# Spline attention: the exponents of a row block in two pieces of 1568 columns instead of four of 784

## The reference, cut to what matters

```python
q, k, v = (x projected by Wq, Wk, Wv)          # 4 heads of 32, 3136 pixels
sim  = einsum('bhnd,bhdm->bhnm', q, k) / sqrt(32)
xs   = clip(sim, -6, 6)
kan  = base_w * silu(xs) + einsum('...k,k->...', b_splines(xs), coef)   # cubic splines, knots 2.4 apart
attn = softmax(kan, axis=-1)                   # over the 3136 keys
out  = einsum('bhnm,bhmd->bhnd', attn, v)
return einsum('bihw,ci->bchw', out, Wo)
```

## Time and profile before

| what | value |
|---|---|
| median of three runs | 8487.42 us |
| profiled execution, its own time | 8486.63 us |
| its span | 8484.9 us |
| busy share PE / DVE / ACT / POOL | 79% / 77% / 69% / 64% |
| mean granted TensorE clock | 0.916 |

### The profile page before, as it was taken

The page is one execution under the profiler, slowest core; times in us unless marked ns, Lnnn a source line. Parts: engine busy times, 40 slices in busy tenths (PEclk is TensorE's granted clock), DMA queues, the critical chain, the costliest instruction groups (busy, mean ns, idle before and its releaser), DMA issues. The chain is left out here.

```text
span 8484.9 us, 160875 instructions
## 1 busy us (share of the span) xinstructions
PE 6665.1 (79%) x52568; PEld 4066.2 (48%) x52568; DVE 6493.4 (77%) x8488; ACT 5894.8 (69%) x8624; POOL 5438.2 (64%) x3590
## 2 busy tenths in 40 slices
PE   5676689989678888876888888688888867888886
PEld 3444447767544444443444444344444434444443
DVE  3323374444489999987999999499999969999997
ACT  4325002223189999986999899399999958999996
POOL 3314000000088888876888888388888858888885
PEclk7788799999899999998999999799999989999998
DMA  1000000000100000001000000200000010000001
GB/s 64 17 11 27 0 0 0 0 0 0 47 8 0 0 0 0 0 2 29 0 0 0 0 0 0 62 1 0 0 0 0 0 31 1 0 0 0 0 0 39
DMA packets 44706, 72.18 MB, mean 9 GB/s; under 512 B 8928, under 2 KB 40448, under 8 KB 42016
## 3 DMA queue, kind: packets, MB, share of 16 engines
q1 hardware_dynamic: 41296, 70.25, 3.1%
q10 hardware_dynamic: 3288, 0.33, 0.0%
HBM read 50.69 MB, written 19.73 MB: 8 GB/s over the span
## 5 line engine op out<-in xcount | busy, mean ns | idle before, releaser
L1389 POOL TENSOR_TENSOR a_s<-a_s,a_v 128x784 f32<-128x784 f32 x1568 | 2910.2, 1857 | 568.2 <-ACT a_s L1563 521.3
L1425 PE MATMUL a_right_sides<-a_s,diag_d 128*128 128x392 f32 x6272 | 2470.5, 541 | 233.3 <-DVE a_prob L1470 212.8
L1425 PEld LDWEIGHTS a_right_sides<-a_s,diag_d 128*128 128x128 f32 x6272 | 1237.0, 210 | 1074.3 <-issue 420.0
L1497 DVE SCALAR_TENSOR_TENSOR a_kan<-a_s,spline_c,a_kan 128x784 f32<-128x784 f32 x1568 | 1629.5, 1039 | 112.4
L1437 PE MATMUL a_turned<-ident,a_prob 128*112 128x128 f32 x5488 | 937.3, 296 | 854.0 <-ACT a_probT L1570 661.2
L1382 POOL TENSOR_TENSOR a_inner<-a_inner,a_x 128x784 f32<-128x784 f32 x784 | 1453.8, 1854 | 65.4
L1437 PEld LDWEIGHTS a_turned<-ident,a_prob 128*112 128x112 f32 x5488 | 584.3, 138 | 1116.4 <-ACT a_probT L1570 718.2
L1546 ACT ACTIVATE a_a<-a_x 128x784 f32<-128x784 f32 x784 | 672.2, 857 | 509.6 <-DVE a_x L1476 506.8
L1449 PEld LDWEIGHTS a_weighed<-a_probT,a_V 112*64 112x64 f32 x21952 | 755.8, 138 | 491.2 <-issue 434.8
L1449 PE MATMUL a_weighed<-a_probT,a_V 112*64 112x64 f32 x21952 | 945.9, 229 | 0.2
L1507 DVE CUSTOM_DVE_ANT_0 a_prob<-a_kan,a_prob 128x784 f32<-128x784 f32 x784 | 764.1, 975 | 153.9 <-DVE a_kan L1497 153.9
(11 more groups left out here) (182 smaller groups left out, 7840.0 us busy)
## 6 DMA issues: line engine op xcount, KB each, us to landing
rows<-bias_rows_dram SPq DMA_DIRECT2D x112, 91.0 KB
X<-in_x_dram SPq DMA_DIRECT2D x4, 1568.0 KB, 15.0
v_dram<-V SPq DMA_DIRECT2D x14, 448.0 KB, 3.1
a_K<-k_dram SPq DMA_DIRECT2D x8, 784.0 KB, 9.5
QO<-q_dram SPq DMA_DIRECT2D x8, 784.0 KB, 12.8
a_V<-v_dram SPq DMA_DIRECT2D x4, 1568.0 KB, 22.1
f_R<-rinv_dram SPq DMA_DIRECT2D x8, 784.0 KB, 7.6
out_dram<-X SPq DMA_DIRECT2D x4, 1568.0 KB, 10.2
```

The costliest lines, as they stand in the source:

```text
L1389: eng.tensor_tensor(s, s, v, ALU.mult).then_inc(cubed, 1)
L1425: mm = eng.matmul(up[:, j, 0:SUB], steps[i][:, :], cubes[g][:, SUB * j:SUB * (j + 1)], start=(i == 0), stop=(i == 1))
L1497: eng.scalar_tensor_tensor(F, banked((s1, s2)[j][g][:, :]), c[:, 3 + j:4 + j], F, ALU.mult, ALU.add).then_inc(left_added, 1)
```

## The change: what it does

The list of ScalarE has two exponents a step instead of four. `exponent(half)` works on 1568 columns, the quarters 2 x half and 2 x half + 1 of `prob`, and adds 2 to `exp_done`, so that all waits keep their numbers. `exponent(1)` stands where the exponent of quarter 2 stood, `exponent(0)` where that of quarter 0 stood; the entries of quarters 3 and 1 are gone.

```diff
-                def exponent(g):
+                def exponent(half):
                     def stage(eng, t, r):
+                        f = prob[r][:, HALF * half:HALF * (half + 1)]
                         eng.wait_ge(max_ready, t + 1)
-                        eng.activation(part(r, g), part(r, g), ACT.Exp, bias=nmax[r][:, :]).then_inc(exp_done, 1)
+                        eng.activation(f, f, ACT.Exp, bias=nmax[r][:, :]).then_inc(exp_done, 2)
                     return stage
...
-                pipeline(act, TILES3, [(tanh(2), 1), (copies(1), 2), (first_knot(0), 0), (exponent(2), 2), (copies(2), 2), (second_knot(0), 0),
-                                       (tanh(3), 1), (copies(3), 2), (first_knot(1), 0), (exponent(3), 2), (copies(4), 2), (second_knot(1), 0),
+                pipeline(act, TILES3, [(tanh(2), 1), (copies(1), 2), (first_knot(0), 0), (exponent(1), 2), (copies(2), 2), (second_knot(0), 0),
+                                       (tanh(3), 1), (copies(3), 2), (first_knot(1), 0), (copies(4), 2), (second_knot(1), 0),
                                        (tanh(0), 0), (copies(5), 2), (first_knot(2), 0), (exponent(0), 1), (copies(6), 2), (second_knot(2), 0),
-                                       (tanh(1), 0), (copies(0), 1), (first_knot(3), 0), (exponent(1), 1), (place, 2), (second_knot(3), 0)])
+                                       (tanh(1), 0), (copies(0), 1), (first_knot(3), 0), (place, 2), (second_knot(3), 0)])
```

## The result

The changed kernel takes 8520.37 us, the median of six runs (8515.73 to 8523.13), against 8487.19 us before (six runs, 8485.32 to 8491.7): ratio 1.0038, 95% interval 1.0025 to 1.0051, 33 us slower. The forecast was 8549 us, 62 slower, with a range of 8500 to 8595. The profiled execution took 8517.76 us, its span is 8516.0 us, 31.1 more than before.

What follows compares the result with a forecast made beforehand. VectorE was taken to bound the spline attention. Two waits of L1484 (47 us) and the late copy (15 us) made 62 us, so 8487.4 + 62 = 8549 us, with a range of 8500 to 8595.

Steps and rivals of the forecast that it cites:

- What bounds: Spline attention: VectorE is full, ScalarE waits for it; VectorE's work alone makes the block of 29.39 us.
- The saving: ScalarE's exponents: a 1568-column piece takes 1596 ns; 0.36 us less per block, in idle time, counted at nothing.
- ScalarE's wait before Abs: Sign for the profile after: ScalarE's wait before Abs, 509.6 us idle before the change, would be larger.
- The two waits of L1484: VectorE's first addition waits for a later TANH, 0.17 us in quarter 3, 0.08 to 0.09 in quarter 1: 47 us.
- The copy behind TANH of quarter 3: ScalarE's later copy delays TensorE's right side and, in some blocks, TANH of quarter 1: 15 us, from 0 to 60.
- the 19 of the working: Blocks, of 196, in which the prediction saw ScalarE wait for TensorE at the later copy.
- the assumed quarter of all blocks: Share of blocks in which the late copy would delay TANH of quarter 1: 50 x 0.3 = 15 us.
- The waits for right sides: VectorE's waits for TensorE's right sides: near 47.5 us still, over 100 if the clock case is right.
- the late square and cube of quarter 2: ScalarE's second square and GpSimd's cubes are 0.66 us late; additions wanting the cubes come more than a quarter later.
- Hidden: Rival: the margin before L1484 absorbs the longer exponent, 8487 to 8504 us; chance 0.14.
- ScalarE's saving: Rival: ScalarE sets the step, so 0.36 us a block, 71 us, would go: 8417 us; chance 0.04.
- The clock: Rival: TensorE's gap grows from 1.62 to about 2.1 us, lowering its clock; 91 us on top, 8640 us; chance 0.14.

Runs made afterwards that it cites:

- e10b: e7b with pieces of 1008, 1232 and 896 columns, so that the transpose of chunk 2 waits for the second piece: 9372.69 us.
- e1: Kernel before with only the first half as one exponent of 1568 columns; quarters 2 and 3 keep their own: 8487.65 us.
- e2: Kernel before with only the second half as one exponent of 1568 columns; quarters 0 and 1 keep their own: 8508.13 us.
- e3b: Changed kernel with each half as two exponents of 784 columns directly behind each other: 8592.55 us.
- e4: Changed kernel with both exponents of 1568 columns moved ahead of first_knot, where ScalarE would wait for the clip: 8492.04 us.
- e9b: e7b with its first piece moved ahead of first_knot(2): 8490.9 us.
- e7b: Changed kernel with three pieces cut at transposed chunks' edges: 1344 columns at quarter 0's old place, 896 at those of quarters 2 and 3: 8461.55 us.
- e12: e7b with its first 1344 columns as 1008 and 336, so four pieces (1008, 336, 896, 896) at the four old places: 8473.28 us.
- e5: Kernel before with its four exponents of 784 columns each moved ahead of first_knot: 8488.59 us.
- e11b: e7b's three pieces in the kernel before, plus the copy of chunk 1 moved ahead of the TANH of quarter 2: 8496.07 us.
- e6b: Changed kernel with second_knot(2) moved ahead of the exponent of the first half: 8546.72 us.

## Why the prediction was right, and what in it was not

**What bounds.** Right. VectorE has next to no idle time to give in the stages. Every kernel here but e10b is its work plus these two sorts of waits, to within 4 us over the stages.

**The saving.** Right: L1581 takes 1587 ns for the 1596 forecast, and the time saved went into idle time, that before TANH (51.8 us before, 254.1 after). One sign named ahead was wrong: ScalarE's wait before Abs was to be larger and is smaller, 476.8 us for 509.6.

**The two waits of L1484.** Right, and they are the result: 0.17 us forecast for quarter 3 and 0.165 measured, 0.09 for quarter 1 and 0.086 measured. 47 us were forecast and 51.3 measured; the difference is mostly the 30 blocks left out as held before, which were not held any more. The sign was stated in the wrong measure: as idle time the 40 to 50 us forecast are 21.0, as start-to-start time 51.3. e1 and e2 show either half by itself, e3b the same sum at 0.84 us, e4 and e9b that nothing is left of it where the exponent stands before the clip's wait.

**The copy behind TANH of quarter 3.** This step failed, 15 us forecast. In 11 blocks L1484 of quarter 1 was over 0.1 us later than in the others, 2.1 us in all. In the kernel before ScalarE waited at that copy in 11 blocks and not in the 19 of the working, and none came on top, so the assumed quarter of all blocks was 50 for 11.

**What wasn't in the sum.** The waits for right sides were taken as fixed ("near 47.5 us still"), and they went, 18 us. I had the late square and cube of quarter 2 in the working and looked only for whom they hold up, which is TensorE (104.8 us of waits) but never VectorE through it. That heavy work placed later might keep TensorE's clock up just after was not asked.

**The time.** It came out at 33 us for 62, just over half: 15 us too much for the copy and 18 for the waits that went, against 4 too few for L1484. The direction and the larger term are right by their mechanism.

**The rivals.** Hidden fell with e3b and both halves. ScalarE's saving fell: e4 has the shorter ScalarE and no late TANH, and is at 1.0001; the rule of the Trainium skill ("ScalarE: Activation LUTs", section on what ACT_TABLE_LOAD costs) holds for the instruction (1587 ns for 1568 columns, 933 for 784) and not for the step. The clock mattered, but the other way. The gap before the right side of quarter 0, on which this rival stood, did not grow to 2.1 us: where it is long it is about 1.6 us before and after, and the waits before that gate did not grow at all. The Trainium skill ("TensorE: Matmul & The Clock Gate", section on HAM oscillation) warns of idle gaps between bursts of matmuls. That gaps matter the trace bears out, though the gaps of that section's example are longer than the 1.6 to 2.2 us here. But of the two here only the one before quarter 3 cost something, and the longer gap did not cost the more: before its transpose TensorE is idle 1.85 us (median) in the kernel before, with 30 waits, and 2.16 in the changed one, with 2.

**Still open.** Theory D rests on the swap of e9b, on e7b, and on the times of e12; it is a rule found in this kernel, and how the clock decides is not shown. The time from the end of the right side of quarter 2 to the start of that of quarter 3 goes with it in the main: 5.38 to 5.43 us (medians) in the kernel before, e4, e5 and e9b, with 23 to 36 waits, 4.67 to 4.76 in the changed kernel, e1, e3b and e7b, with 2. But e12 has 5.05 with 17 waits and e2 5.24 with 12, so it is not the whole. That e2 has 12 waits and not 30, with an early cube, is not explained. e7b and e12 are 9 and 7 us faster than their account; over the stages of the profiled executions it is 4 and 2, and the rest lies outside them or between executions. Why e11b's waits appear before quarter 0 was not tried further; that low-clock stretches have a new place there is only argued from its start of the right side.

## What to carry to other kernels

A longer instruction on an engine that is not the bottleneck is priced by one number: what it adds between the last thing its engine waits for and the next deadline of the bottleneck engine, less the margin seen there; 0.65 us against margins of 0.49 and 0.57 came out to 0.01 us. Ahead of the wait such work costs the bottleneck engine nothing (e4, e9b); behind it, it has to fit the margin (e7b). Cut it so that no consumer waits for a later piece than it needs: that is all the cut itself did here, as 1344 + 896 + 896 takes 8462 us in one place and 8491 in another. And where results of TensorE are just in time, as the right sides here, the order and the times of its light and heavy work can decide over its clock, so look at the granted clock after a change that moves them, and don't add up two improvements that both do.

## What the runs showed of the hardware

With the same work on TensorE, the granted clock over 2400 to 8400 us was 0.95 in e7b and 0.92 in e9b, which differ by the swap of two entries in ScalarE's list. Eight matmuls of a right side take 2.80 us at the upper level and 5.31 where it was at the lower one nearly throughout. Busy time in this stretch, first e7b, then e9b (columns as in the earlier trace rows):

```profile
2400.00:8400.00 6000.00, 4767.72 (x39929) 2699.47 (x39930) 5428.60 (x6684) 5132.82 (x6813) 5078.12 (x3299) 0.95 0.02 4
```

```profile
2400.00:8400.00 6000.00, 4810.43 (x39742) 2762.58 (x39742) 5410.27 (x6656) 5133.01 (x6789) 5080.43 (x3291) 0.92 0.02 4
```

An exponent of 1568 columns in place costs 1587 ns, one of 784 costs 933, so 0.834 ns a column. L1484 starts 0.03 us (median) after the end of a TANH that it waits for, in e1, e2, e3b, e6b and the changed kernel.
